# A fused two-layer decoder on one core: packed head outputs with row sums from ScalarE in the second many-head stage, and a block mask moved from TensorE to DMA and VectorE

## The reference, cut to what matters

```python
x = x + L0_attn(layernorm(x))                     # stage 0: one head
x = x + L0_xattn(layernorm(x), ctx, mask)         # stage 1: 16 heads of 16, masked
x = x + L0_ffn(layernorm(x))                      # stage 2
x = x + L1_attn(layernorm(x))                     # stage 3: 16 heads of 16, no mask
x = x + L1_xattn(layernorm(x), ctx, tokens)       # stage 4: 16 heads of 16, masked
x = x + L1_ffn(layernorm(x))                      # stage 5: 8 experts, 2 per token, and a shared one
```

```python
attn  = softmax(q @ k.T / 4)                      # per head, 128 x 128
heads = attn @ v                                  # per head, 128 x 16
out   = heads.reshape(128, 256) @ w_o.T + b_o + x # x is the normed input of the part
```

## Time and profile before

| | |
|---|---|
| time, median of 3 runs | 791.42 us (790.24 to 791.65) |
| the profiled execution: its time | 791.41 us |
| its span (first to last instruction) | 789.6 us |
| busy: PE, PE weight loads | 755.5 us (96%), 615.4 us (78%) |
| busy: DVE, ACT, POOL | 521.3 us (66%), 425.0 us (54%), 330.8 us (42%) |
| chain that ended last: PE, DVE, issue, POOL, ACT, DMA | 63%, 17%, 7%, 7%, 4%, 2% |
| DMA | 61.46 MB, mean 78 GB/s |
| granted PE clock | 0.996 |

### The profile page before, as it was taken

The page is one execution under the profiler, slowest core; times in us unless marked ns, Lnnn a source line. Parts: engine busy times, 40 slices in busy tenths (PEclk is TensorE's granted clock), DMA queues, the critical chain, the costliest instruction groups (busy, mean ns, idle before and its releaser), DMA issues.

```text
span 789.6 us, 17005 instructions
## 1 busy us (share of the span) xinstructions
PE 755.5 (96%) x6045; PEld 615.4 (78%) x6045; DVE 521.3 (66%) x1418; ACT 425.0 (54%) x1254; POOL 330.8 (42%) x457
## 2 busy tenths in 40 slices
PE   7999999999899999999999999999999999999997
PEld 6887777776688888877777777777777767888886
DVE  4675788887622343137767767788899987567655
ACT  2445677777532222337777766677665667323320
POOL 3233333443323222314222216666678745715550
PEclk9999999999999999999999999999999999999999
DMA  8902234322042226000000003000000001235539
GB/s 312 390 5 75 75 100 120 79 75 75 15 134 74 74 78 145 14 1 2 1 2 2 2 2 121 15 15 15 15 15 28 28 29 48 87 96 162 162 109 319
DMA packets 57569, 61.46 MB, mean 78 GB/s; under 512 B 21296, under 2 KB 48176, under 8 KB 56464
## 3 DMA queue, kind: packets, MB, share of 16 engines
q1 hardware_dynamic: 54080, 51.03, 21.2%
q0 software_dynamic: 3408, 9.34, 3.5%
HBM read 31.10 MB, written 29.27 MB: 76 GB/s over the span
## 4 chain that ended last, share of the span: by engine, by line
PE 63%; DVE 17%; issue 7%; POOL 7%; ACT 4%; DMA 2%; SPq 1%; POOLq 0%; DVEq 0%; ACTq 0%
PE pj L366 8%; PE pj L373 8%; PE pj L460 7%; PE ov L536 7%; PE sc L523 7%; PE sc L449 6%; DVE mx L1005 5%; POOL routed_y L1770 5%; PE ov L471 4%; PE pj L360 4%; DVE pT L1012 2%; PE sc L444 2%; ACT pr L1499 2%; PE sc L666 2%; DVE sc L998 2%
## 5 line engine op out<-in xcount | busy, mean ns | idle before, releaser
L1499 ACT ACTIVATE pr<-sc,mx 128x128 f32<-128x128 f32 x768 | 216.6, 395 | 82.3 <-DVE mx L1005 80.1
L1005 DVE TENSOR_REDUCE mx<-sc 128x4 f32<-128x512 f32 x192 | 125.6, 683 | 38.5 <-PE sc L449 36.4
L460 PE MATMUL pj<-idn,pr 128*128 128x128 f32 x768 | 121.3, 283 | 5.4 <-DVE pT L1012 1.3
L460 PEld LDWEIGHTS pj<-idn,pr 128*128 128x128 f32 x768 | 83.9, 141 | 44.5 <-issue 24.9
L1012 DVE COPY pT<-pj 128x512 f32<-128x512 f32 x128 | 87.1, 686 | 31.9 <-PE pj L460 31.6
L1687 POOL TENSOR_SCALAR ve<-mv 128x2 f32<-128x2 f32 x40 | 14.1, 352 | 185.4 <-DVE mv L936 184.9
L1517 ACT ACTIVATE hT<-sc,vecs 128x256 f32<-128x256 f32 x64 | 30.3, 473 | 90.6 <-PE sc L523 90.6
L523 PE MATMUL sc<-xnT,W 128*128 128x256 f32 x256 | 64.1, 380 | 0.0
L536 PE MATMUL ov<-W,hT 128*128 128x256 f32 x256 | 60.5, 381 | 0.0
L449 PE MATMUL sc<-kM,qT 32*128 32x256 f32 x768 | 55.0, 400 | 4.4 <-ACT pr L1499 4.0
L1482 ACT ACTIVATE pT<-pj 128x512 f32<-128x512 f32 (+1 forms) x72 | 42.0, 585 | 27.6 <-PE pj L460 27.0
(11 more groups left out here) (227 smaller groups left out, 1537.1 us busy)
## 6 DMA issues: line engine op xcount, KB each, us to landing
sorted_x<-more_xT SPq DMA_DIRECT2D x15, 1152.0 KB, 6.9
kM<-sorted_x SPq DMA_DIRECT2D x39, 129.0 KB, 2.1
cT<-in_ctxT SPq DMA_DIRECT2D x16, 256.0 KB, 3.4
W<-in_w SPq DMA_DIRECT2D x2, 1024.0 KB, 13.6
cT<-in_ctx SPq DMA_DIRECT2D x8, 256.0 KB, 3.0
W<-in_w_gu SPq DMA_DIRECT2D x1, 2048.0 KB, 8.0
hT<-routed_y SPq DMA_DIRECT2D x8, 256.0 KB, 5.7
out_x<-X SPq DMA_DIRECT2D x8, 256.0 KB, 3.9
```

The costliest lines, as they stand in the source:

```text
L460: last = tr(bank[b][:, i * S:(i + 1) * S], pr[n % 4][:, i, :], idn[:])
L1005: v.tensor_reduce(mx[n % 4][:], four(b), AX.X, ALU.max, negate=True).then_inc(mx_done, 1)
L1499: last = a(pr[n % 4][:, i, :], bank[b][:, i * S:(i + 1) * S], ACT.Exp, bias=mx[n % 4][:, i:i + 1])
```

## The change

In stage 3:

- Two heads share 32 rows. The values of even heads stand in columns 0 to 15 of their 32, those of odd heads in columns 16 to 31, the rest is zero (POOL clears it once before the stage). Two matmuls add into one place, so `O` is 128 x 256 and already has feature rows in a permuted order; the weights and the bias are permuted on the host to fit.
- There is no column of ones. Each `Exp` has an `accum_out` that writes its row sum to `hsum`, and DVE makes the inverses, each written 16 times (`spread_inv`, 128 x 256, `inverse_sums`). PE turns these (two transposes per half) in place of the outputs, and DVE multiplies `oT` by them straight into `hdT`. `turn_heads` and ACT's copy to `hdT` are gone from this stage.
- DVE copies all eight groups of turned probabilities (`ACT_TURNS[3] = ()`); ACT's copy of `O` is half as wide.
- `exps(U, n)` waits until the inverses of the unit before have read the sums; POOL sets the ones again for stage 4.

In stage 2:

- The bf16 mask matmuls are gone. The mask (now 1 for kept, float32, 16 rows x 256) is copied by ACT at the end of the unit before, written by SP to DRAM (`kept_at`), and read back by eight DMAs of 64 partitions x 2 rows, each row repeated over 64 partitions (`spread`), into `pr` or `pT`, which are unused in the stage.
- DVE multiplies the hidden values by it, four times 128 x 512 a unit (`keep_hidden`), at the end of the unit; for units 18 to 23 the first of the four stands at the head of `alone0`.
- `down2` waits for these products; `hidden2` waits for the `down2` of two units before.

Elsewhere: the load of the mask matrix (512 KB) and its cast on DVE in unit 6 are gone; the routed rows have one semaphore for a pair.

```diff
@@ PE
-                mm(bank[b][:, 0:T], expb[:, c * P:(c + 1) * P], nmT[U % 2], start=True, stop=False)
                 for d in range(C):
                     last = mm(bank[b][:, 0:T], W1[:, d, c * P:(c + 1) * P], xnT[U % 3][:, d, :],
-                              start=False, stop=d == C - 1)
+                              start=d == 0, stop=d == C - 1)
...
-                    pe.wait_ge(*emptied("h", U, d))
+                    pe.wait_ge(kept_hidden, 4 * (U % PAIRS) + d // 2 + 1)
...
+                    if stage(U) == 3:
+                        for i in range(4):
+                            last = mm(bank[b][32 * i:32 * i + 32, g // 2 * S:(g // 2 + 1) * S],
+                                      va[U % 2][:, j, 2 * (g // 2 * 4 + i) + g % 2, :], pT[g][:, i, :],
+                                      start=g % 2 == 0, stop=g % 2 == 1, skip_group_check=True)
+                        continue
...
+                if stage(U) == 3:
+                    pe.wait_ge(ri_done, 2 * att(U) + j + 1)
+                    for k in range(C):
+                        inverse = spread_inv[j][:, 8 * k:8 * k + 8, :].rearrange("p u d -> p (u d)")
+                        last = tr(bank[b][:, k * S:(k + 1) * S], inverse, idn[:])
+                    last.then_inc(filled[b], 1)
+                    return
...
-                        pe.wait_ge(s_routed[2 * p + j], 16)
+                        pe.wait_ge(s_routed[p], 32)
...
-                if stage(U - 1) in (3, 4):
+                if stage(U - 1) == 4:
                     turn_heads(U - 1)
@@ DVE
+            def inverse_sums(U, j):
+                dve.wait_ge(*emptied("s", U, 4 * j + 3))
+                v.reciprocal(spread_inv[j][:], along(hsum[j][:].rearrange("p c i two -> p (c i two)"), DH)).then_inc(ri_done, 1)
...
+                if stage(U) == 3:
+                    dve.wait_ge(*emptied("O", U, j))
+                    dve.wait_ge(filled[b], k)
+                    v.tensor_tensor(hdT[U % 2][:, :, j * S:(j + 1) * S], oT[j][:, 0:C, :],
+                                    bank[b][:, 0:T].rearrange("p (c s) -> p c s", c=C), ALU.mult).then_inc(drained[b], 1)
+                    return
...
+            def keep_hidden(U, q):
+                p = U % PAIRS
+                if q == 0:
+                    dve.wait_ge(s_keep[U % 2], 128 * (p // 2 + 1))
+                dve.wait_ge(*emptied("h", U, 2 * q + 1))
+                some = hT[U % 2][:, 2 * q:2 * q + 2, :]
+                v.tensor_tensor(some, some, keep[U % 2][q], ALU.mult).then_inc(kept_hidden, 1)
...
             def part0(U):
+                if stage(U - 1) == 3:
+                    inverse_sums(U - 1, 1)
...
             def part3(U):
+                if stage(U) == 3:
+                    inverse_sums(U, 0)
...
             def alone0(U):
+                if stage(U) == 2 and U % PAIRS >= 2:
+                    keep_hidden(U, 0)
...
             def alone1(U):
+                if stage(U) == 2:
+                    for q in range(int(U % PAIRS >= 2), 4):
+                        keep_hidden(U, q)
...
-                if U == 6:
-                    dve.wait_ge(s_w[2], 64)
-                    v.tensor_copy(expb[:], expd).then_inc(s_bf, 1)
@@ ACT
-        ACT_TURNS = {1: (2, 6), 3: (2, 6), 4: (1, 2, 5, 6)}
+        ACT_TURNS = {1: (2, 6), 3: (), 4: (1, 2, 5, 6)}
...
+                if stage(U) == 3 and U > 3 * PAIRS:
+                    act.wait_ge(ri_done, 2 * att(U - 1) + n // 4 + 1)
                 for i in range(4):
-                    last = a(pr[n % 4][:, i, :], bank[b][:, i * S:(i + 1) * S], ACT.Exp, bias=mx[n % 4][:, i:i + 1])
+                    total = hsum[n // 4][:, n % 4 // 2, i, n % 2:n % 2 + 1] if stage(U) == 3 else None
+                    last = a(pr[n % 4][:, i, :], bank[b][:, i * S:(i + 1) * S], ACT.Exp, bias=mx[n % 4][:, i:i + 1],
+                             accum_out=total)
...
             def part3(U):
...
+                if stage(U + 1) == 2:
+                    if (U + 1) % PAIRS >= 2:
+                        act.wait_ge(s_kept, 16 * ((U + 1) % PAIRS - 1))
+                    copy_out(nmT[(U + 1) % 2], "nm", U + 1)
@@ SP
+            def spread(U):
+                p = U % PAIRS
+                sp.wait_ge(*emptied("nm", U))
+                sp.dma_start(kept_at[p], nmT[U % 2][0:NB, :]).then_inc(s_kept, 16)
+                sp.wait_ge(s_kept, 16 * (p + 1))
+                if p == 0:
+                    sp.wait_ge(*full("pT", U - 1, 7))
+                elif p == 1:
+                    sp.wait_ge(*full("O", U - 2, 1))
+                else:
+                    sp.wait_ge(kept_hidden, 4 * (p - 1))
+                for h in two:
+                    rows_of = kept_at[p].rearrange("(c h) t -> h c t", h=2)[h]
+                    for i, some in enumerate(keep[U % 2]):
+                        sp.dma_start(some[h * BLOCK:(h + 1) * BLOCK], rows_of[2 * i:2 * i + 2].unsqueeze(0)
+                                     .to_broadcast([BLOCK, 2, T])).then_inc(s_keep[U % 2], 16)
```

More of the change, by code:

```diff
@@ L68, with program @@
 NROW = sum(n for _, n in ROWS.values())
-def program(nc, x, ctxT, ctx, tokq, tokk, mask, ident, causal, expand, vec, rows, lnb, before, blank,
+def program(nc, x, ctxT, ctx, tokq, tokk, mask, ident, causal, vec, rows, lnb, before, blank,
             w_qk, w_ov, w_q0, w_k0, w_v0, w_r0, w_1, w_2, w_qkv, w_o1, w_x, w_g, w_gu,
-            w_down, ws_gate, ws_up, ws_down, sorted_x, routed_y, out):
+            w_down, ws_gate, ws_up, ws_down, kept_at, sorted_x, routed_y, out):
     stack = ExitStack()
@@ L146, in program @@
         rin = [sb(f"rin{r}", [P, H]) for r in two]
+        hsum = [sb(f"hsum{r}", [P, 2, 4, 2]) for r in two]
+        spread_inv = [sb(f"spread_inv{r}", [P, H, DH]) for r in two]
         hd = [sb(f"hd{r}", [P, 2, D]) for r in two]
@@ L206, in program @@
         nm = sb("nm", [P, 2, P])
-        nmT = [mask4[:].rearrange("p b s -> p (b s)").bitcast(BF16)[:, r * T:(r + 1) * T] for r in two]
+        nmT = [mask4[:].rearrange("p b s -> p (b s)").bitcast(F32)[:, r * T:(r + 1) * T] for r in two]
+        keep = [[t[:].rearrange("p a s -> p (a s)").rearrange("p (c t) -> p c t", t=T) for t in ring] for ring in (pr, pT)]
         sg = [t[:].rearrange("p j s -> p (j s)") for t in sh]
@@ L269, in program @@
         s_yt = [sem(f"s_yt{r}") for r in range(4)]
-        s_routed = [sem(f"s_routed{b}") for b in range(B)]
+        s_routed = [sem(f"s_routed{p}") for p in range(PAIRS)]
+        s_kept, kept_hidden = sems("s_kept kept_hidden")
+        s_keep = [sem(f"s_keep{r}") for r in two]
         sg_done = sem("sg_done")
-        ACT_TURNS = {1: (2, 6), 3: (2, 6), 4: (1, 2, 5, 6)}
+        ACT_TURNS = {1: (2, 6), 3: (), 4: (1, 2, 5, 6)}
         DVE_MASKED = {1: (2, 3, 6, 7), 3: (), 4: (3, 7)}
@@ L567, in output3 @@
                 pe.wait_ge(drained[b], n - 1)
-                pe.wait_ge(*emptied("hT", U))
+                for j in two:
+                    pe.wait_ge(*emptied("OT", U, j))
                 along_tokens(b, hdT[U % 2], Wo1)
@@ L1037, in values @@
                 else:
-                    bias = R({1: "bv0", 3: "bv1"}[W // PAIRS]).rearrange("p (h d) -> p h d", h=H)
+                    if W // PAIRS == 3:
+                        if W < 3 * PAIRS + 2:
+                            dve.wait_ge(s_two, 2 * (W % PAIRS) + 2)
+                        for j in two:
+                            side = va[W % 2][:, j].rearrange("p (u two) (a d) -> p u (two a) d", two=2, d=DH)[:, :, 0::3, :]
+                            last = v.tensor_tensor(side, bank[b][:, j * D:(j + 1) * D].rearrange("p (u two d) -> p u two d", two=2, d=DH),
+                                                   R("bv1").rearrange("p (u two d) -> p u two d", two=2, d=DH), ALU.add)
+                        last.then_inc(drained[b], 1)
+                        return
+                    bias = R("bv0").rearrange("p (h d) -> p h d", h=H)
                     v.tensor_tensor(dst, src, bias.unsqueeze(1).to_broadcast([P, 2, H, DH]),
@@ L1516, in hidden2 @@
                 act.wait_ge(filled[b], n)
+                if c == 0 and U % PAIRS >= 2:
+                    act.wait_ge(*full("y2", U - 2))
                 a(hT[U % 2][:, c, :], bank[b][:, 0:T], ACT.Relu, bias=V("b1", c)).then_inc(drained[b], 1)
@@ L1578, in dense @@
                 if stage(U) == 2:
-                    if m == 0 and not attends(U - 1):
-                        copy_out(nmT[U % 2], "nm", U)
                     hidden2(U, 2 * m)
@@ L1773, in slot @@
             def slot(U, m):
+                if U == 2 * PAIRS + 4 and m == 0:
+                    pool.wait_ge(*full("O", 2 * PAIRS - 1, 1))
+                    for r in two:
+                        g.memset(va[r][:, :, 0::2, DH:DH + 1], 0.0).then_inc(s_two, 1)
+                        g.memset(va[r][:, :, 1::2, 0:DH], 0.0).then_inc(s_two, 1)
+                if U in (4 * PAIRS - 1, 4 * PAIRS) and m == 2:
+                    pool.wait_ge(*full("O", U - 1, 1))
```

(7 more changed lines are left out.)

38 lines of the change are left out of this document (20 added, 18 removed).

## The result

In 13 runs of each, the changed kernel took 793.37 us in the median (791.37 to 795.3) and the kernel before 791.12 (789.93 to 792.6): ratio 1.0023, 95% interval 1.0012 to 1.0033. In a later series it was 793.82 against 791.62, 1.0038 (1.0023 to 1.0053). So it is slower, as forecast, but by about 2 us (2.2 by the medians) and not by 4.8. The ratios are those on record with their intervals; they are not the quotients of the medians beside them and differ from these by up to 0.16%.

What follows compares the result with a forecast made beforehand. PE was taken to bound stage 2, and in stage 3 the second half of a unit, ACT's Exp loop the first. Stages 2 and 0 -6.8, stage 3 +10.9, end +0.7: +4.8, so 796.2 us, range 788 to 804.

Steps and rivals of the forecast that it cites:

- Exps with a sum: Stage 3, ACT: accumulator reads add 0.145 us an Exp, 4.6 us a unit; first half 9.9 us against 8.81, +1.1.
- The second half of a unit: Stage 3: DVE's passes sum to 9.6 us, over the loop (8.7) and PE (8.56), so DVE bounds it, +0.4.
- Unit 24: Start of stage 3: first half, mostly `down2` matmuls, +0.6 us; second half, 7.3 before, takes DVE 8.8, +1.5.
- units 30 and 31: Stage 3 units carrying stage 4 projections: unit 30 +1.1 and -0.5 us by halves, unit 31 +0.2 and -0.5.
- The mask: Stage 2: dropping 64 mask matmuls gives -6.9 us; products late for unit 16's mask cost +0.7.
- the margin: Stage 2, units 18 to 23: mask reads land at +8 us and may land until +10.8 before PE feels it.
- The cast: Stage 0: the mask's cast, 0.66 us between two steps of DVE's chain, goes: -0.6 us.
- The end: End of program: PE's first routed product of pair 5 waits for both sequences' row sets, not one: +0.7 us.
- cheap inverses: Rival, stage 3: wide reciprocal takes 0.42 us, a unit 18.6, total -1.9 us, 789.5; chance 0.09.
- hidden accumulators: Rival, stage 3: accumulator reads add nothing from PSUM, first half 8.6 us, total about -2, 789.3; chance 0.06.
- stay the bound of stage 3: Rival: DVE and ACT have room, so PE decides: -0.88 us a unit, total about -13, 778; chance 0.09.
- Late mask: Rival, stage 2: mask reads slower than 50 ns a packet; 802 us at twice the time, over 825 at three; chance 0.14.

Runs made afterwards that it cites:

- the ledger: Both kernels, unchanged, profiled once more and compared by stage, with the half clock at 205.6 to 209.0 us taken off the kernel before: sum +1.5 us.
- three small edits: Changed kernel with a reciprocal of 16 sums then a spreading copy, query scaling on DVE, and three products ahead of the folded pieces: 781.82 against 791.62 us, 0.9874.
- the control: Kernel before with only the scaling and bias of stage 3's queries moved from ACT to DVE: 789.28 against 793.46 us, ratio 0.9960.

## Why the prediction was wrong

The direction was right, and each of the two engines that it named (ACT in the first half, DVE in the second) stands on the chain of its half. The size was off by 3.3 us by the ledger, the rest of two larger errors of opposite sign: 6 us too much loss in stage 3, 3 us too much gain in stage 2. That the total came as near as this is luck. The step that failed is the length of a steady unit of stage 3: a price of the Exps that was too high, and a sum of DVE's passes where a chain decides.

*Exps with a sum.* Forecast 0.395 us from one to the next, from stage 0; measured 0.345. Sixteen in a half make 0.8 us, and the first half of 9.9 becomes 9.1; it is 9.23. The mechanism was right, and the price was mis-sized: it was taken from another form of the instruction (the Exps of stage 0, whose source is in SBUF) because the trace of before has no nearer row. The bounds should have reached down towards the 0.25 of the earlier trace rows; only a rival without any cost stood there.

*The second half of a unit.* Forecast 9.6 us as the sum of DVE's passes; measured 9.23. Here the step itself was wrong, and not only a size. DVE was busy 8.45 us, and taking 0.61 of it away changed nothing. The half is a chain that goes through PE's queue, one copy and the reciprocal, and back to PE; moving the reciprocal by 5 us in DVE's queue shortened it by 0.33. A sum of busy time is a bound on an engine without gaps, and DVE had gaps: it waits for scores and for transposes. The reciprocal itself was well sized (1.74 for 1.9); the copy of 0.61 was costed on a path that it isn't on.

Together these two are the steady unit, 18.46 for 19.5: 5 x 1.04 = 5.2 us of the 6. Unit 24 (+1.8 for +2.1) and the first half of unit 32 (+1.0 for +1.2) came as forecast, though the second half of unit 32 gave 0.4 back; units 30 and 31 came out even (+0.6 and -0.3 forecast).

*The mask.* Forecast -6.9 + 0.7; measured -3.3. The mask matmuls are worth what was said: units without a wait are 0.89 us shorter (16.26 to 15.36, for example), 8 x 0.111. But the first stall was seen too small and a second kind not at all. The reads were priced by their packets, 3.2 + 2.1 = 5.3 us; the packets took about 50 ns, as said, but the sum has no term for SP, which issues a read each 0.65 us, and from the first issue to the last landing it is 7.7 to 9.4 us. In unit 16 the write of 16 KB with its wait took 2.6 to 3.4 us besides, not the 2.1 of the earlier trace rows. So the mask of unit 16 is late in five of nine profiles, and PE's two waits and restarts in unit 17 then cost 2.0 us (0.7 otherwise, as forecast). Unit 16 itself became 0.41 us shorter and not 0.89 (11.50 to 11.09). (The short unit 17 is no gain to be had: in all four profiles that show it half clock had held unit 16 back, by 1.4 us in the first, and the mask came in time for that.) And the products of units 18 and 20 stand in DVE's queue behind the fold, 0.5 and 0.85 us; I had counted the queue behind the products, and not what stands ahead of them. In units 18 to 23 DVE waits 22.3 us for masks in all, 3.7 a unit, and PE doesn't pay: the margin held.

*The cast.* Forecast -0.6, measured 0: 196.61 and 196.65. The 0.9 us between the first profiles at this place was half clock at 18 us in one of them.

*The end.* PE's wait for the routed rows is 1.40 us against 0.80 in the second profiles, +0.6 for +0.7.

The rivals: cheap inverses and hidden accumulators were each wrong in their premise, but the truth on the sums lay between the forecast and the second. PE did not stay the bound of stage 3: it is idle for 1.5 us of a steady unit. Late mask came true in unit 16 alone, at 2 us, and not by slow packets.

The medians differ by 2.2 us and the ledger by 1.5. The kernel runs at half clock somewhat longer; kernels with the changed stage 3 show such a stretch at 361 to 366 us in two of nine profiles, and none of the four others does. That the rest of the difference comes from there is possible and not shown.

## What to carry to other kernels

When work moves to an engine with idle time, follow the one chain that ends last through the queues of both engines and ask where in the queue the new step stands; the busy sum of the engine gives neither the bound nor the gain (here one reciprocal, moved in its queue, was worth more than a whole copy taken away). A wait that an engine has today (ACT's 0.6 us for the queries) is the room that new work may fill for nothing, so it belongs in the sum. Small reads have a price at the engine that issues them, beside that of their packets. The change lost by 0.2 to 0.4%; with three small edits in the queues that it had loaded it is 1.3% faster than the kernel before, of which the control gets 0.4% without the change.

## What the runs showed of the hardware

**Row sums.** From PSUM, an Exp of 128 elements with a sum starts 0.34 us after the last, without a sum 0.25; the read of the accumulator is shown as 0.19 to 0.32 us but lies mostly under the next Exp.

**Reciprocal.** 1742 ns for 256 elements and 243 for 16: (1742 - 243) / 240 = 6.2 ns an element; a copy of the same 256, spread from 16, takes 330. The Trainium skill ("VectorE: DVE Perf Modes", the walkthrough of the 8-slice pipeline) gives a repeat count of 8, which makes 8.3 ns an element as an estimate at 0.96 GHz; the trace shows a quarter less.

**DVE beside GpSimd.** Four products of two SBUF inputs took 2.49 us alone and 4.64 beside two additions of GpSimd, which were themselves 1.64 and 1.72 us long in place of 1.27; two of the four products took 1.75 us each, the other two 0.68. These rows of DVE and of GpSimd are from the first profile of the changed kernel:

```profile
216.25 4.64 DVE L1128 TENSOR_TENSOR hT<-hT,pr 128x512 f32<-128x512 f32 x4
...
231.69 2.49 DVE L1128 TENSOR_TENSOR hT<-hT,pT 128x512 f32<-128x512 f32 x4
```

```profile
216.42 1.64 POOL L1805 TENSOR_TENSOR X<-X,hd 128x512 f32<-128x512 f32 x1
218.02 1.72 POOL L1799 TENSOR_TENSOR X<-X,rws 128x512 f32<-128x512 f32 x1
```

The Trainium skill ("SBUF — State Buffer", two separate sides) says that a DVE operation with two SBUF inputs and a GpSimd operation that reads SBUF take turns at a shared pair of ports, each holding it for the whole instruction; the trace agrees, with 2.15 us lost by DVE.

**Half clock.** In the thirteen profiles PE's granted clock fell to 1.2 GHz for 3.4 us at a time, at 16 to 23, 203 to 209, 361 to 366 and 660 to 680 us, in each profile at one to four of these places, and for 0.2 to 3.6 us at the end of each. PE had been idle shortly before: at 201 to 205 us for 1.84 and 0.25 us, at 359 to 361 for 2.06. The same idle time stands at 201 to 205 us in the two profiles whose clock did not fall there (it fell in eleven). At 361 too it stands in profiles whose clock did not fall, both of the changed kernel among them. A stretch cost 1.39 us at 205 and 1.6 in each of the two profiles at 362; each figure is a comparison of two single profiles.

**A small write and its reads.** In units 20 to 22 a write of 16 KB to DRAM and the wait for it took 1.4 to 1.5 us from SP's issue of the write to the first read. In unit 17 it took up to 6.7 us: in the second profile of the changed kernel it landed at 223.60 us, just after the table rows (1152 and 9 KB) that SP had issued 2.4 and 1.9 us before it, which landed at 222.39 and 223.40, and after a 16 KB packet of q8. SP needs 5.2 us or more to issue eight reads of 128 KB to 64 partitions each, 0.65 us apiece, and in unit 16 the last lands 2.6 to 4.0 us later. As the issue sets the pace, no run shows what the transfers alone would take.
